# Attention block on one core: the values' high part, ones column and low part side by side, one 129-column product where there were two

## The reference

```python
x_n = group_norm(x)                              # 32 groups
q, k, v = conv1x1(x_n, wq, bq), conv1x1(x_n, wk, bk), conv1x1(x_n, wv, bv)
q, k, v = to_heads(q), to_heads(k), to_heads(v)  # 4 heads of 64 channels
attn = softmax(einsum('bhqd,bhkd->bhqk', q, k) * 64 ** -0.5)
out = einsum('bhqk,bhkd->bhqd', attn, v)
return x + conv1x1(out, wp, bp)
```

## Time and profile before

| | |
|---|---|
| median of the runs shown | 367.16 us (366.61 to 367.82, 3 runs) |
| the profiled execution's own time | 366.61 us |
| its span in the trace | 364.9 us |
| TensorE products (PE) | busy 348.4 us, 95% of the span, 4581 instructions |
| TensorE weight loads (PEld) | busy 209.4 us, 57% |
| VectorE (DVE) | busy 283.2 us, 78%, 445 instructions |
| ScalarE (ACT) | busy 302.1 us, 83% |
| GpSimd (POOL) | busy 284.2 us, 78% |
| granted TensorE clock | 1.000, the 2.4 GHz level |

### The profile page before, as it was taken

The page is one execution under the profiler, slowest core; times in us unless marked ns, Lnnn a source line. Parts: engine busy times, 40 slices in busy tenths (PEclk is TensorE's granted clock), DMA queues, the critical chain, the costliest instruction groups (busy, mean ns, idle before and its releaser), DMA issues.

```text
span 364.9 us, 11249 instructions
## 1 busy us (share of the span) xinstructions
PE 348.4 (95%) x4581; PEld 209.4 (57%) x4581; DVE 283.2 (78%) x445; ACT 302.1 (83%) x361; POOL 284.2 (78%) x258
## 2 busy tenths in 40 slices
PE   0999999999999999999999999999999999999996
PEld 0634564655656565655666556565656556655564
DVE  4889899878888687878887777777877787787474
ACT  1748879998887999989877999988889888888982
POOL 5064989699778998988778998988979797967722
PEclk9999999999999999999999999999999999999999
DMA  6046241123743440261643342031552451060113
GB/s 206 25 131 160 45 97 38 31 91 85 135 129 74 93 98 31 29 184 38 131 146 66 72 88 70 8 82 43 117 164 50 96 91 60 2 203 2 31 31 118
DMA packets 38731, 30.92 MB, mean 85 GB/s; under 512 B 23820, under 2 KB 31512, under 8 KB 38680
## 3 DMA queue, kind: packets, MB, share of 16 engines
q1 hardware_dynamic: 37936, 29.15, 32.8%
q10 hardware_dynamic: 744, 1.06, 0.8%
HBM read 9.44 MB, written 4.19 MB: 37 GB/s over the span
## 4 chain that ended last, share of the span: by engine, by line
PE 84%; DVE 9%; ACT 2%; issue 2%; DMA 1%; DVEq 1%; POOL 0%; ACTq 0%
PE gen L612 19%; PE st L734 13%; PE st L735 13%; PE pv L757 9%; PE pv L760 8%; PE pv L759 7%; PE st L702 5%; PE mx L702 3%; DVE mx L1003 3%; PE st L612 2%; DVE p_lo L1029 2%; PE mx L815 1%; ACT st L924 1%; DVE mx L999 1%; DMA xin<-in_x_dram 1%
## 5 line engine op out<-in xcount | busy, mean ns | idle before, releaser
L919 ACT ACTIVATE p_hi<-st 128x1024 f16<-128x1024 f32 x127 | 130.7, 1029 | 41.2 <-PE st L735 40.6
L1268 POOL TENSOR_TENSOR p_lo<-p,p_hi 128x1024 f16<-128x1024 f32 x62 | 132.2, 2132 | 10.2 <-ACT p L924 10.2
L757 PEld LDWEIGHTS pv<-v_hi,p_hi 128*128 128x128 f16 x1024 | 93.4, 97 | 26.7 <-issue 14.7
L757 PE MATMUL pv<-v_hi,p_hi 128*128 128x65 f16 x1024 | 106.5, 195 | 0.3 <-DVE o L1037 0.2
L759 PE MATMUL pv<-v_lo,p_hi 128*128 128x64 f16 x1024 | 106.0, 193 | 0.0
L760 PE MATMUL pv<-v_hi,p_lo 128*128 128x65 f16 x1024 | 105.8, 194 | 0.0
L1029 DVE TENSOR_TENSOR p_lo<-st,p_hi 128x512 f16<-128x512 f32 x126 | 80.9, 684 | 31.6 <-ACT st L924 31.3
L734 PE MATMUL st<-q_twice,k_both 128*128 128x512 f16 x256 | 97.1, 379 | 1.6 <-DVE p_lo L1029 1.2
L759 PEld LDWEIGHTS pv<-v_lo,p_hi 128*128 128x128 f16 x1024 | 93.9, 99 | 6.2
L735 PE MATMUL st<-q_max,k_one 65*128 65x512 f16 x256 | 97.3, 380 | 0.0
L760 PEld LDWEIGHTS pv<-v_hi,p_lo 128*128 128x128 f16 x1024 | 93.9, 97 | 0.0
(11 more groups left out here) (183 smaller groups left out, 545.0 us busy)
## 6 DMA issues: line engine op xcount, KB each, us to landing
q_twice<-st_hi_q SPq DMA_DIRECT2D x64, 64.0 KB, 2.1
xres<-in_x_dram SPq DMA_DIRECT2D x4, 1024.0 KB, 5.2
out_dram<-y SPq DMA_DIRECT2D x13, 256.0 KB, 2.3
xin<-in_x_dram SPq DMA_DIRECT2D x6, 512.0 KB, 4.7
k_both<-st_hi_k SPq DMA_DIRECT2D x16, 128.0 KB, 2.3
k_one<-st_hi_k SPq DMA_DIRECT2D x16, 128.0 KB, 2.6
q_max<-st_lo_q SPq DMA_DIRECT2D x32, 64.0 KB, 2.1
k_both<-st_lo_k SPq DMA_DIRECT2D x16, 128.0 KB, 2.3
```

The lines of the kernel that those rows point to most:

```text
L757: nc.tensor.matmul(pv_v[:, q, :], hi, vh, start=k == 0 and q == 0, stop=False, skip_group_check=True)
L919: nc.scalar.activation(p_hi[:, G % PR, :, :], scores, ACT.Exp, scale=SM_SCALE / M_SCALE)
L1268: nc.gpsimd.tensor_tensor(p_lo[:, G % PR, :, :], p_full(G), p_hi[:, G % PR, :, :], ALU.subtract)\
```

## The change

`v_hi` and `v_lo` become slices of one tensor `v_all` with 129 columns per chunk and head: 64 high, the constant, 64 low. For query tiles 0 to 2 (MERGED = 3) one 129-column product with `p_hi` replaces the 65-column and the 64-column one; its low columns get their own place in PSUM, so a query tile's stride there is 129 instead of 65. Four such tiles make 516 columns, over the 512 of a bank, so tile 3 keeps three products and uses 65 columns; all that is written lies in the first bank of a two-bank tensor whose second bank is the old `gen`. The two statistics' columns move behind the new layout. VectorE now has to add the low columns of tiles 0 to 2: `divide` takes the reciprocals, drains, multiplies the low columns (128x192) into `o_low`, drains, and then makes four instructions of 64 columns, three that multiply the high columns and add `o_low` and one that only multiplies.

```diff
+    MERGED = QT - 1
...
-        v_hi = sb("v_hi", [P, CT, NK, 2, PV], F16)
-        v_lo = sb("v_lo", [P, CT, NK, 2, D], F16)
+        v_all = sb("v_all", [P, CT, NK, 2, PV + D], F16)
+        v_hi = v_all[:, :, :, :, 0:PV]
+        v_lo = v_all[:, :, :, :, PV:PV + D]
...
+        o_low = sb("o_low", [P, MERGED, D])
...
-        pv = pb("pv")
-        gen = pb("gen")
+        pv_gen = pb("pv_gen", 2)
+        pv, gen = pv_gen[:, 0:512], pv_gen[:, 512:1024]
...
-        pv_v = pv[:, 0:QT * PV].rearrange("p (t n) -> p t n", n=PV)
+        pv_v = pv_gen[:, 0:QT * (PV + D)].rearrange("p (t n) -> p t n", n=PV + D)
...
-            first = QT * PV + (0 if kind == "mean" else CT)
+            first = MERGED * (PV + D) + PV + (0 if kind == "mean" else CT)
...
+                    both = v_all[:, head // 2, k, head % 2, :]
                     for q in range(QT):
...
-                        nc.tensor.matmul(pv_v[:, q, :], hi, vh, start=k == 0 and q == 0,
-                                         stop=False, skip_group_check=True)
-                        nc.tensor.matmul(pv_v[:, q, 0:D], hi, vl, start=False, stop=False, skip_group_check=True)
-                        last = nc.tensor.matmul(pv_v[:, q, :], lo, vh, start=False,
+                        if q < MERGED:
+                            nc.tensor.matmul(pv_v[:, q, :], hi, both, start=k == 0 and q == 0,
+                                             stop=False, skip_group_check=True)
+                        else:
+                            nc.tensor.matmul(pv_v[:, q, 0:PV], hi, vh, start=False, stop=False, skip_group_check=True)
+                            nc.tensor.matmul(pv_v[:, q, 0:D], hi, vl, start=False, stop=False, skip_group_check=True)
+                        last = nc.tensor.matmul(pv_v[:, q, 0:PV], lo, vh, start=False,
                                                 stop=k == NK - 1, skip_group_check=True)
...
-                then(nc.vector.reciprocal(rden[:, U % 2, :], pv_v[:, :, D]))
-                nc.vector.tensor_tensor(o32[:, half, :, (U % 2) * D:(U % 2 + 1) * D], pv_v[:, :, 0:D],
-                                        rden[:, U % 2, :].unsqueeze(2).to_broadcast([P, QT, D]), ALU.mult)\
-                  .then_inc(s_o32, 1)
+                divide(U, half, (range(QT),))
+
+            def divide(U, half, parts):
+
+                columns = slice((U % 2) * D, (U % 2 + 1) * D)
+                share = rden[:, U % 2, :]
+                then(nc.vector.reciprocal(share, pv_v[:, :, D]))
+                then(nc.vector.tensor_tensor(o_low[:, :, :], pv_v[:, 0:MERGED, PV:PV + D],
+                                             share[:, 0:MERGED].unsqueeze(2).to_broadcast([P, MERGED, D]), ALU.mult))
+                for tiles in parts:
+                    for t in tiles:
+                        if t < MERGED:
+                            last = nc.vector.scalar_tensor_tensor(out=o32[:, half, t, columns], in0=pv_v[:, t, 0:D],
+                                                                  scalar=share[:, t:t + 1], in1=o_low[:, t, :],
+                                                                  op0=ALU.mult, op1=ALU.add)
+                        else:
+                            last = nc.vector.tensor_scalar(o32[:, half, t, columns], pv_v[:, t, 0:D],
+                                                           share[:, t:t + 1], None, ALU.mult)
+                    last.then_inc(s_o32, 1)
```

More of the change, by code:

```diff
@@ L1045, in normalise_last @@
                 wait(dve, s_o_lo, U // 2 - 1)
[L1046 to L1051, removed]
+                divide(U, 1, (range(0, 2), range(2, QT)))
             def channel_stats(b, t, parts=(0, 1)):
```

## The result

The changed kernel takes 381.05 us (median of 4 runs, 380.78 to 383.17) against 366.99 us before: a ratio of 1.0386, 95% interval 1.0361 to 1.0410. It is slower by 14.1 us. I had forecast 373.5 us with a range of 369.5 to 378: the direction is right, the size is under half of what happened (6.5 of 14.1 us), and the time lies outside the range.

A forecast was written before the change was run, and what follows sets the result against it. TensorE was taken as the bound for two thirds of the time. From 366.6 us, 8.4 us of division costs less 1.7 us of counted saving gave 373.3, set at 373.5 us half-way to the median's basis; range 369.5 to 378.

The forecast's parts named there:

- the least gap of 0.06 us: Between the division's end on VectorE and TensorE's next L757: the signal's own way, 0.06 us, expected almost everywhere after the change.
- four instructions of 64 columns: Last part of VectorE's new division: no drain between, starts 0.14 us apart, three times making 0.42 us.
- the last one's own duration: End of the new division: the last 64-column instruction takes 0.22 us, from 0.425 us less 192 columns.
- the multiply-and-add form costs what the multiplication does: Price of the division's multiply-and-add instructions on VectorE, taken from 416 ns for 256 columns out of PSUM.
- the same table: TensorE's waits by unit, each 0.65 + 0.06 - gap, 23 units at mean gap 0.52 us; 8.4 us with the tail.
- the tail: After the last division, TensorE's transposes wait for tiles 0 and 1, out at 1.04 us instead of 0.54: 0.5 us.
- small losses: In a slot's weighing, a few ns where a load isn't ready, 0.023 us per slot, mostly at the merged pair.
- Faster: Rival: gaps before the next weighing cover the division if it lengthens by less than about 0.4 us; 364.5 us, chance 0.08.
- extra: How much later the division's sums come than before: 0.65 us, with bounds of 0.5 and 0.8 us.
- The small instructions don't overlap: Rival: each 64-column instruction starts when the one before has ended, four take 0.88 us, waits 16 us; 382 us, chance 0.05.
- The merge saves nothing but six fixed parts: Rival on TensorE's weighing: 0.9 us counts instead of 1.7; 374.1 us, inside the forecast's range, no separate chance.
- my own bound: Upper bound: sums 0.8 us later give 13 us of waits and a time of 378.6 us.

The follow-up runs named there:

- e3: Against the changed kernel, a constant in place of the per-partition scalar in the four 64-column instructions; 373.69 us, ratio 1.0175.
- e2_division_only: Against the kernel before, its three products kept but the new division used, with high columns fed as low ones; 382.40 us, ratio 1.0418.
- e1: Against the changed kernel, merged products kept but the division of before, low columns' sums left out; 365.21 us against 367.43 us, ratio 0.9941.

## Why the prediction was wrong

**Right:** that TensorE is the bound and the division its new wait; 3813 products; the reciprocal, the 192 columns and the drain to 0.01 us; the least gap of 0.06 us at nearly every unit; that about half of TensorE's saving is lost in that wait (1.0 of 2.2 us by the ratios, 0.9 of 2.0 us in the traces).

**The step that failed** is "four instructions of 64 columns": "0.067 + 0.075 = 0.14 us, three times 0.42 us" and "the last one's own duration ... 0.22 us". They measure 0.19 us and 0.276 us, together 0.86 us instead of 0.64, and the last step of it makes 0.87 us of the forecast's 0.65. The mechanism was right; this term of the sum was too small by 0.22 us. I took the overhead of neighbours from instructions with an immediate scalar or a second tensor and wrote that "the multiply-and-add form costs what the multiplication does". That is true with an immediate scalar, as in the row it rests on the earlier trace rows, and the constant in e3 shows it again (215 ns). The change's scalar is an operand in SBUF, 60 ns more each. No row that I used had one.

**How it grew.** With 0.87 us in place of 0.65 the same table gives: 23 units x (0.93 - 0.52) = 9.4 less 0.4; two at 0.81, 1.6; three at 0.87 and one at 0.5, 3.1; 0.5, 0.4, and 0.75 for the tail: 15.4 us in place of 8.4. The error of 0.22 us was multiplied by some 32 units, because beyond the gap of 0.5 us nothing is hidden any more. The first 0.65 us cost 8.4 us, the next 0.22 us another 7. `e2_division_only`, `e3_immediate` and the changed kernel bear this table out, at 382.4, 373.7 and 381.05 us.

**A second size.** TensorE's saving is 2.2 us and not 3.8 (e1), close to the 1.9 us that six fixed parts of 2.5 ns alone make. The "small losses" that I let go with the merged pair stay: the weighing takes 0.71 us and not the 0.70 of the forecast. Counted at half, it is 1.0 us instead of 1.7. Two readings behind the 3.8 us were wrong. I took the 9% of L757 in the chain, against 8% and 7%, for small losses at the merged pair. The chain in order of time shows what they are, the first product of a weighing behind the maxima products:

```profile
72.36 0.22 PE mx L702 x2
72.57 0.14 PE pv L757
72.86 0.03 PE pv L757
```

There are 53 such pieces of over 0.1 us, 7.3 us in all or 2% of the span, about the surplus of L757, and the merge leaves that step as it is: in most slots where a maxima product comes last, the weighing's first product starts 0.31 us after it in the kernel before and in `e1_products_only`. The pair's small losses mostly stay with the merged product: from start to start, in the mean between 75 and 310 us, the pair inside a weighing took 31.9 + 29.2 = 61.1 ns and the 129-column product takes 58.1 ns, while tile 3's three products went from 90.9 to 93.6 ns.

The sum on the profiled execution's basis becomes 366.6 + 15.4 - 1.0 = 381.0 us, where it took 380.8.

**The rivals.** *Faster* needed an extra under 0.4 us: e1, with no extra, is faster by 0.6%, so the mechanism was there and the number was not. *The small instructions don't overlap* is wrong as a mechanism, but it pointed at the right term: they overlap by 0.08 us each (start 0.19 us apart, 0.276 us long), and its price of 382 us lay above the result only because little of the saving was taken off; by the working's own terms, 366.6 + 16 - 1.7, it is 381 us, the measured time. A number that fits does not make the mechanism right, and here it got a chance of 0.05. *The merge saves nothing but six fixed parts* is what happened, on top of the forecast's case. **The range** took 0.8 us as the upper end of the extra; the measured 0.87 lies outside it, and I let the high end of the range stop at 378 although my own bound was 378.6. (Its terms, 366.6 + 13 - 1.7, give 377.9, so the bound rests on the 0.8 us alone.) The bound should have come from asking which operand kinds the new instructions have that no row has.

One smaller slip: VectorE's "83%" divides by the old span; by the forecast's longer one it is 82%. The 80% measured belong to a span of 379 us. Nothing hung on it.

## What to carry to other kernels

When an engine that is the bound waits at a shared buffer, price the path from "last written" to "free again", not the busy time of the engine that frees it: here VectorE was busy 80% and a lengthening of 0.24 us on that path (`e3_immediate` against the changed kernel) still cost 7.4 us. Take data out of the shared bank first and compute afterwards; that turned 1.039 into 0.997. Many short instructions each pay their fixed part, so look at each operand's kind (scalar in SBUF, second tensor in SBUF) before taking a price from a row that looks alike.

## What the runs showed of the hardware that I had not expected

- A per-partition scalar operand in SBUF costs VectorE 60 ns per instruction, in duration and in spacing alike: 276 against 215 ns for 64 columns, for the multiply-and-add and the plain multiplication.
- A VectorE instruction with two SBUF operands lasted up to 2.18 us instead of 0.36 while a GpSimd instruction ran, and ended 0.20 to 0.22 us after it in 24 cases of 24; with one operand in PSUM it lasted 0.36 us each time.
- In the kernel with those waits the granted clock fell to 0.58 for a stretch of 3.4 us after TensorE had been idle for 2 of 5.6 us. In the changed kernel, where TensorE idled 0.2 to 0.75 us before each unit's weighing, it stayed at 1.00 from 75 to 310 us.
